# Row maxima of an attention kernel found bank by bank, its head projection taken out within one group, one product moved to GpSimd

## The chip, the cores and the metric

One core of a Trainium2 chip runs the whole program. The metric is the time of one execution in microseconds (us) of device time. The kernel before took 4465.28 us (median of three runs, 4464.08 to 4466.0). Engines are named PE (TensorE), PEld (its weight loads), DVE (VectorE), ACT (ScalarE), POOL (GpSimd) and SP (SyncE).

## The reference

A decoder layer in fp32 on x of shape (2, 2048, 512): self-attention, cross-attention to 77 rows, and a feed-forward block in which a router sends 512 rows of each batch through a larger network. The change lies in the self-attention, which is this:

```
x = x + attn(layernorm(x))
q, k, v = (h @ W.T).reshape(B, S, H, DK)        # H = 16 heads, DK = 64, S = 2048, B = 2
scores  = einsum('bhqd,bhkd->bhqk', q, k) + rel_bias[bucket(k - q)]
attn    = softmax(scores, axis=-1)
out     = einsum('bhqk,bhkd->bhqd', attn, v)  -> @ Wo.T
```

`rel_bias` is a table of 32 buckets by 16 heads. A key more than 128 columns before or after its query always falls in one of two buckets, so the bias is a constant there ("far"); nearer than that it varies ("near").

## The kernel before, in words

The program has three parts: `attention` (self-attention), `middle` (cross-attention and the light network), `routed` (the router and the heavy network). Only `attention` is changed. Each engine has its own instruction stream, written out by hand; semaphores tie them together. Nothing is reordered by a scheduler, so an instruction that waits holds up all that is behind it on its engine.

**Heads and groups.** Batch and head together make 32 units, called heads here, numbered 0 to 31. `heads` calls `head(n)` for n from -2 to 31 on every engine. A head is 32 steps (`STEPS`): two halves of 1024 queries, and in each the 16 tiles of 128 keys. Two steps make a group, so a head has 16 groups, g = 0 to 15. Three heads are in work at once: head n has its scores, exponentials and values; the row maxima of head n+1 are found in groups 3 to 15 of head n and the last three query tiles in groups 0 to 2 of the next; the projection of queries and keys of head n+2 is computed in four blocks of 512 columns, each over the groups 4b+1, 4b+2 and 4b+3. Head -2 so does only projection, head -1 projection and maxima.

**One group on PE** (`head` at L502) is, in order: score products "low" of step 2g, each with a product for a row maximum beside it (`row_tiles`, L472; low uses rows 64 to 127 of the array at L470, the maximum rows 0 to 63 at L455); "high" products of steps 2g and 2g+1 (L469; in groups 0 and 8 preceded by "first", L467, and there without low); a third of a projection block (L441, in three groups of four); low and maximum of step 2g+1; eight value products of the two steps before (L490, four matmuls of two instructions). Groups 4 and 12 end with the column sums of a finished half (`sum_of`, L499 and L500), which write the bank PB. The projection uses the same bank PB, so `sum_of` also waits until the block in it has been taken out (semaphore `step_lo`).

**Row maxima.** For each of 16 query tiles, four matmuls of 512 keys each give the raw scores, two at a time ("pair" 0 and 1 of a group) into the two banks MX and MX+1. DVE reduces both banks in one instruction of 1024 columns (`largest`, L726). PE's first matmul of the next pair waits for that reduction (`max_done`). `guards` (L728) makes of eight tiles' maxima the subtrahend of the softmax, `neg_max`, in two instructions (L732, L737); the second also subtracts the head's largest bias.

**Exponentials.** ACT waits for `scored`, and for near tiles for `biased`, which DVE's `near` (L747) signals; it writes `probs`, a ring of four steps. POOL adds `probs` into `acc` (L227, L230), 30 additions a head. PE's "high" of step 2g+1 waits for the exponential of step 2g-1.

**Taking out a projection block.** In groups 3, 7, 11 and 15, ACT copies the queries (`queries_out`, L598) between its two exponentials and the keys twice (`keys_out`, L602 and L603) after the second; DVE makes the queries' low part at the group's end (L753). In the group after it (4, 8, 12, 0), DVE forms the difference of keys two tiles apart (`step`, L759), ACT copies it (`step_hi`, L608), DVE makes its low part (`step_lo`, L765).

**Context.** When a half is done, its sums go through SP's DMAs to be inverted (`reciprocals`, L772, groups 13 and 5) and come back; DVE multiplies the context by them (`context`, L778, groups 14 and 6), and SP stores it.

Lines to follow: `row_tiles` and `max_half` (PE), `queries_out`, `keys_out`, `step_hi` (ACT), `largest`, `guards`, `step`, `step_lo`, `context` (DVE).

Of the kernel before, what the change touches and what calls it, by code (L numbers as in the profile page):

```python
# [71 lines left out]
CONTEXT_GROUPS = {14: 0, 6: 1}  # L72
# [11 lines left out]
def attention(nc, io, scr):  # L84

    with ExitStack() as c:
# [3 lines left out]
        def sem(name):  # L90
# [30 lines left out]
        maxes = sb("maxes", [P, NT, 2])  # L121
        max_q = sb("max_q", [P, NT])
# [20 lines left out]
        names = """const_ready consts_in bias_table bias_mm bias_stored wv_in wv_hi wv_lo stat  # L143
            moment rstd1 rstd2 xn turned xhi xlo vps vout w_in w_hi w_split
            proj q_hi k_own k_hi q_lo step step_hi step_lo fill_max fill_score
            maxed max_done neg1 neg_ready neg_stored neg_in
# [45 lines left out]
        def _(pool):  # L192
# [17 lines left out]

            def head(n, k, side):
# [6 lines left out]
                for st in range(STEPS):  # L218
                    qb, kt = divmod(st, NT)
                    if kt == 0:  # L220
                        continue
# [10 lines left out]
            heads(pool, head)  # L232

        @block.sync
        def _(sp):
# [28 lines left out]
            sp.wait_ge(s["bias_table"], 3)  # L264
# [123 lines left out]
        def _(pe):  # L388
# [57 lines left out]
            def max_half(n, side, g, pair, i):  # L446

                late, qt = max_tile(g)
                m, mside = (n + 1, 1 - side) if late else (n, side)
                if i == 0:  # L450
                    if late and g == FIRST_MAX and pair == 0:
                        pe.wait_ge(s["fill_max"], FILLS_MAX * (m + 1))
                    past(pe, s["max_done"], NT * 2 * m + 2 * qt + pair)
                kc = 2 * pair + i
                mm = pe.matmul(ps[:, MX + i, :], stacks[0:64, mside, QA, qt * P:(qt + 1) * P],  # L455
                               stacks[0:64, mside, KX, kc * 512:(kc + 1) * 512], start=True, stop=True)
                if i == 1:
                    mm.then_inc(s["maxed"], 1)
# [92 lines left out]
        def _(act):  # L551
            act.wait_ge(s["bias_mm"], 1)
            act.copy(rtab, ps[0:H, MX, :]).then_inc(s["bias_table"], 1)
# [37 lines left out]
            def queries_out(m, tb):  # L591
# [7 lines left out]

            def keys_out(m, tb):  # L600

# [38 lines left out]
            def head(n, k, side):  # L640
                carry, own, nxt, prep = parts(n)
                for g in range(GROUPS):
# [4 lines left out]
                    if prep and g in EVAC_GROUPS:  # L647
                        queries_out(n + 2, EVAC_GROUPS[g])
                    if g in SPLIT_GROUPS:
                        tb = SPLIT_GROUPS[g]  # L650
                        if tb < BLOCKS - 1 and prep:
                            step_hi(n + 2, tb)
                        if tb == BLOCKS - 1 and nxt:
                            step_hi(n + 1, tb)
                    if own:
                        exp(n, k, side, 2 * g + 1)
                    if prep and g in EVAC_GROUPS:
                        keys_out(n + 2, EVAC_GROUPS[g])
# [14 lines left out]
        def _(dve):  # L673
            dve.wait_ge(s["consts_in"], 48)
            dve.tensor_copy(rconst[:, 0:2], rb_t[:, FAR_AFTER:BUCKETS:BUCKETS // 2]).then_inc(s["bias_table"], 1)
            dve.memset(rconst[:, 3:4], 0.0)
            dve.tensor_reduce(rconst[:, 2:3], rb_t[:], AX.X, ALU.max).then_inc(s["bias_table"], 1)
# [42 lines left out]
            def largest(n, side, g, pair):  # L720
# [3 lines left out]
                at = NT * 2 * m + 2 * qt + pair  # L724
                dve.wait_ge(s["maxed"], at + 1)
                dve.tensor_reduce(maxes[:, qt, pair:pair + 1], ps[:, MX:MX + 2, :], AX.XY, ALU.max).then_inc(s["max_done"], 1)  # L726

            def guards(m, k, side, half):  # L728

                q = slice(half * 8, half * 8 + 8)  # L730
                dve.wait_ge(s["max_done"], NT * 2 * m + NT * (half + 1))
                dve.tensor_reduce(max_q[:, q], maxes[:, q, :], AX.X, ALU.max).then_inc(s["neg1"], 1)  # L732
                dve.wait_ge(s["neg1"], 2 * m + half + 1)
                if half == 0:
                    dve.wait_ge(s["far_in"][side], k * 16 + 16)
                past(dve, s["neg_stored"], 16 * (2 * m + half - 1))
                dve.tensor_scalar(neg_max[:, q], max_q[:, q], -1.0, far_bias[:, side, 2:3], ALU.mult, ALU.subtract).then_inc(s["neg_ready"], 1)  # L737
# [36 lines left out]
            def context(n, qb):  # L774

# [973 lines left out]
```

## Time and profile before

| | us |
|---|---|
| median of three runs | 4465.28 |
| the profiled execution | 4465.17 |
| its span, first to last instruction | 4463.4 |
| PE busy | 4052.3 (91%) |
| POOL busy | 2617.0 (59%) |
| DVE busy | 2602.8 (58%) |
| ACT busy | 2054.8 (46%) |
| granted TensorE clock, mean | 0.958 of full |

An engine's busy time is the time in which at least one of its instructions is in work. A matmul's recorded length holds its latency, so neighbouring ones overlap and the distance of two starts is what a matmul costs. Times in rows count from the span's start. The stretch in which heads 0 to 31 are worked on lasts from about 338 to 3122 us. A row of a timeline may stand for several instructions of one line (x2, x4), and then starts with the first and ends with the last.

### The profile page before, as it was taken

What the parts mean: (1) busy time and instruction counts of PE and PEld (TensorE: products, weight loads), DVE (VectorE), ACT (ScalarE), POOL (GpSimd) and SP (SyncE); (2) the same over time, 40 slices, a digit from 0 to 9 for tenths busy, and PEclk for the clock granted to TensorE, in tenths of its full rate; (3) what the DMA queues carried; (4) which work ended last, traced back from release to release, by engine and by line L of the source; (5) the groups of instructions that cost most, each with busy time, mean ns of one, the idle gap of its engine ahead of it and who ended that gap; (6) DMA issues with size and microseconds to landing.
All of it is one profiled execution on the core that took longest, in us unless ns stands there. A gap on an engine that the chain in (4) does not pass through costs nothing. (4 is left out here: it accounts for less than half of the span.)

```text
span 4463.4 us, 59267 instructions
## 1 busy us (share of the span) xinstructions
PE 4052.3 (91%) x18676; PEld 2172.5 (49%) x18676; DVE 2602.8 (58%) x3421; ACT 2054.8 (46%) x3407; POOL 2617.0 (59%) x1279
## 2 busy tenths in 40 slices
PE   8969999999999999999999999998588988883599
PEld 6734444444444444444444444443466666662244
DVE  3336666766766676666667667663256666653400
ACT  2215555555555555555555555554234444441110
POOL 1007888888888788888888888888222222220100
PEclk9969999999999999999999999999799999995799
DMA  6522222321222342122223212220311111112100
GB/s 195 147 69 60 72 55 58 93 57 52 81 72 54 111 115 58 52 76 75 57 55 97 57 52 79 71 54 15 116 46 53 53 47 59 47 33 88 38 10 10
DMA packets 340399, 299.90 MB, mean 67 GB/s; under 512 B 188779, under 2 KB 230251, under 8 KB 339304
## 3 DMA queue, kind: packets, MB, share of 16 engines
q1 hardware_dynamic: 272360, 275.94, 21.8%
q10 hardware_dynamic: 66048, 16.78, 1.7%
q0 software_dynamic: 1920, 6.29, 0.5%
q8 instruction: 38, 0.62, 0.1%
q14 instruction: 33, 0.27, 0.0%
HBM read 117.71 MB, written 64.54 MB: 41 GB/s over the span
## 5 line engine op out<-in xcount | busy, mean ns | idle before, releaser
L230 POOL TENSOR_TENSOR acc<-acc,probs 128x1024 f32<-128x1024 f32 x896 | 2148.6, 2398 | 353.7 <-ACT probs L634 215.5
L726 DVE TENSOR_REDUCE maxes<-ps 128x1 f32<-128x1024 f32 x1024 | 1250.5, 1221 | 650.7 <-PE ps L455 649.2
L637 ACT ACTIVATE probs<-ps,far_bias 128x1024 f32<-128x1024 f32 (+7 forms) x1280 | 1023.2, 820 | 1059.4 <-DVE near_s L747 552.4
L490 PE MATMUL ps<-probs,v_head 128*64 128x512 f32 x4096 | 997.0, 608 | 2.1 <-ACT probs L634 2.1
L455 PE MATMUL ps<-stacks 64*128 64x512 f32 x2048 | 759.8, 451 | 37.4 <-DVE maxes L726 37.4
L470 PE MATMUL ps<-stacks 64*128 64x512 f32 x1792 | 662.1, 447 | 0.0
L469 PE MATMUL ps<-stacks 128*128 128x512 f32 x2048 | 617.0, 418 | 0.1
L470 PEld LDWEIGHTS ps<-stacks 64*128 64x128 f32 x1792 | 271.0, 184 | 528.3 <-issue 358.6
L490 PEld LDWEIGHTS ps<-probs,v_head 128*64 128x64 f32 x4096 | 248.9, 136 | 484.1 <-issue 481.1
L469 PEld LDWEIGHTS ps<-stacks 128*128 128x128 f32 x2048 | 350.3, 188 | 215.6 <-issue 163.7
L747 DVE TENSOR_TENSOR near_s<-ps,near_bias 128x384 f32<-128x384 f32 (+2 forms) x576 | 284.1, 493 | 221.9 <-PE ps L470 205.4
L455 PEld LDWEIGHTS ps<-stacks 64*128 64x128 f32 x2048 | 306.8, 188 | 142.9 <-DVE maxes L726 105.5
L634 ACT ACTIVATE probs<-near_s 128x384 f32<-128x384 f32 (+2 forms) x576 | 271.1, 471 | 0.0
L441 PE MATMUL ps<-xn_hi,w_hi 128*128 128x512 f32 x512 | 211.3, 413 | 20.6 <-DVE c_k L765 15.8
L441 PE MATMUL ps<-xn_hi,w_lo 128*128 128x512 f32 x512 | 209.8, 410 | 0.0
L441 PE MATMUL ps<-xn_lo,w_hi 128*128 128x512 f32 x512 | 209.8, 410 | 0.0
L227 POOL TENSOR_TENSOR acc<-probs 128x1024 f32<-128x1024 f32 x64 | 152.9, 2388 | 81.5 <-ACT probs L637 64.9
L417 PE MATMUL ps<-stacks,xn_hi 128*128 128x512 f32 x512 | 163.8, 401 | 11.4 <-DVE xn_lo L703 11.4
L1011 POOL TENSOR_TENSOR m_rs<-m_rs,m_expo 128x1 f32<-128x1 f32 x32 | 17.6, 551 | 258.1 <-DVE m_rs L1245 258.1
L1019 POOL TENSOR_TENSOR m_rs<-m_rs,m_expo 128x1 f32<-128x1 f32 x32 | 17.6, 549 | 230.1 <-DVE m_rs L1245 230.1
L1000 POOL TENSOR_TENSOR m_ctx_lo<-m_ctx,m_ctx_hi 128x1024 fp32r<-128x1024 f32 x32 | 78.5, 2453 | 98.2 <-ACT m_ctx_hi L1176 98.2
L1421 POOL DMA_INDIRECT out<-r_y,index x8 | 7.8, 978 | 215.2 <-DVE r_y L1650 215.2
(222 smaller groups left out, 5046.7 us busy)
## 6 DMA issues: line engine op xcount, KB each, us to landing
stacks<-c_k SPq DMA_DIRECT2D x128, 256.0 KB, 2.4
stacks<-c_q SPq DMA_DIRECT2D x128, 256.0 KB, 2.5
stacks<-c_d SPq DMA_DIRECT2D x256, 128.0 KB, 2.3
scr_v<-c_k ACTq DMA_DIRECT2D x32, 512.0 KB, 4.0
stacks<-c_q SPq DMA_DIRECT2D x128, 128.0 KB, 2.3
v_head<-scr_v SPq DMA_DIRECT2D x32, 512.0 KB, 3.5
sums<-scr_inv SPq DMA_DIRECT2D x128, 128.0 KB, 2.9
scr_ctx<-ctx_out SPq DMA_DIRECT2D x128, 128.0 KB, 2.3
```

The costliest lines, as they stand in the source:

```text
L227: pool.tensor_tensor(acc[:, qb, :], probs[:, (st - 1) % PT_RING, :], pr, ALU.add).then_inc(s["summed"], 2)
L230: pool.tensor_tensor(acc[:, qb, :], acc[:, qb, :], pr, ALU.add).then_inc(s["summed"], 1)
L417: mm = pe.matmul(ps[:, 2 + v % 4, :], xs[i][:, k, t * P:(t + 1) * P], (wv_hi, wv_lo)[j][:, k, half * 512:(half + 1) * 512], start=at == 0, ...
L441: mm = pe.matmul(ps[:, PB, :], w[wi][:, kk, :], xs[xi][:, kk, tb * 512:(tb + 1) * 512], start=a == 0, stop=a == len(TERMS) - 1)
L455: mm = pe.matmul(ps[:, MX + i, :], stacks[0:64, mside, QA, qt * P:(qt + 1) * P], stacks[0:64, mside, KX, kc * 512:(kc + 1) * 512], start=T ...
L469: return pe.matmul(out, stacks[:, side, KA, keys], stacks[:, side, QA, q], start=False, stop=True, skip_group_check=True)
L470: return pe.matmul(out, stacks[64:128, side, KX, keys], stacks[64:128, side, QB, q], start=False, stop=True, skip_group_check=True)
L490: mm = pe.matmul(ps[64 * half:64 * half + 64, PV, :], v_head[:, side, kt, :], probs[:, st % PT_RING, half * 512:(half + 1) * 512], start=k ...
L634: ins = act.activation(probs[:, st % PT_RING, a:z], near_s[:, st % 2, 0:z - a], ACT.Exp)
L637: ins = act.activation(probs[:, st % PT_RING, a:z], sc[:, a:z], ACT.Exp, bias=bias)
L726: dve.tensor_reduce(maxes[:, qt, pair:pair + 1], ps[:, MX:MX + 2, :], AX.XY, ALU.max).then_inc(s["max_done"], 1)
L747: dve.tensor_tensor(near_s[:, st % 2, 0:z - a], sc, near_bias[:, side, j0:j0 + z - a], ALU.add).then_inc(s["biased"], 1)
```

## The change

Four things change, all in `attention`:

1. **Maxima bank by bank.** Every maximum matmul now signals `maxed` and waits for `max_done` of the matmul two before it, which used its bank. `largest` reduces each bank by itself (2048 reductions of 512 columns in place of 1024 of 1024). `guards` is one reduction over four partial maxima.
2. **The largest bias is taken off the tables.** The bias tables have it subtracted once at the start, so `guards` no longer subtracts it and its second instruction (L737) is gone.
3. **The projection is taken out within its group.** ACT does all three copies between its two exponentials and `step_hi` after the second; DVE does `step` right behind `queries_low` at the end of the same group, and `step_lo` between the two near steps of the next group.
4. **The product with the inverted sums is on POOL**, ahead of the addition of steps 30 and 14 (groups 15 and 7).

DVE, from the maxima of the end of group 3 (tile `maxes`) to those of the end of group 4, before: `c_q<-` is the queries' low part, `ps<-ps,c_d` is `step`, `c_k<-` is `step_lo`.

```order
L726 TENSOR_REDUCE maxes<-ps 128x1 [waits a_maxed]
L752 ISA
L753 TENSOR_TENSOR c_q<-ps,c_q 64x512 [waits a_q_hi]
L725 REGISTER_ALU
L726 TENSOR_REDUCE maxes<-ps 128x1 [waits a_maxed]
L743 REGISTER_ALU
L747 TENSOR_TENSOR near_s<-ps,near_bias 128x128 [waits a_scored]
L759 TENSOR_TENSOR ps<-ps,c_d 64x512 [waits a_q_lo,a_k_hi]
L725 REGISTER_ALU
L726 TENSOR_REDUCE maxes<-ps 128x1 [waits a_maxed]
L765 TENSOR_TENSOR c_k<-ps,c_d 64x512 [waits a_step_hi]
```

The same stretch of DVE in the changed kernel, from the second reduction at the end of group 3:

```order
L727 TENSOR_REDUCE maxes<-ps 128x1 [waits a_maxed]
L749 ISA
L750 TENSOR_TENSOR c_q<-ps,c_q 64x512 [waits a_q_hi]
L756 TENSOR_TENSOR ps<-ps,c_d 64x512 [waits a_q_lo,a_k_hi]
L726 REGISTER_ALU
L727 TENSOR_REDUCE maxes<-ps 128x1 [waits a_maxed]
L726 REGISTER_ALU
L727 TENSOR_REDUCE maxes<-ps 128x1 [waits a_maxed]
L740 REGISTER_ALU
L744 TENSOR_TENSOR near_s<-ps,near_bias 128x128 [waits a_scored]
L762 TENSOR_TENSOR c_k<-ps,c_d 64x512 [waits a_step_hi]
```

`step` has moved ahead of the next group's first maxima, and `step_lo` ahead of its last ones (two reductions, which follow).

ACT in groups 3 and 4, before, from the exponential of step 6: `c_q` is the queries' copy, the first `c_d` and the `c_k` the keys', `c_d` with its wait for `step` is `step_hi`.

```order
L634 ACTIVATE probs<-near_s 128x384
...
L598 CAST c_q<-ps 64x512 [waits a_fill_score]
...
L637 ACTIVATE probs<-ps,far_bias 128x768 [waits a_biased]
L634 ACTIVATE probs<-near_s 128x256
L602 COPY c_d<-ps 64x512
L603 CAST c_k<-ps 64x512
...
L637 ACTIVATE probs<-ps,far_bias 128x896 [waits a_biased]
L634 ACTIVATE probs<-near_s 128x128
L608 CAST c_d<-ps 64x512 [waits a_step]
```

And in the changed kernel:

```order
L639 ACTIVATE probs<-near_s 128x384
...
L606 CAST c_q<-ps 64x512 [waits a_fill_score]
L607 COPY c_d<-ps 64x512
L608 CAST c_k<-ps 64x512
...
L642 ACTIVATE probs<-ps,far_bias 128x768 [waits a_biased]
L639 ACTIVATE probs<-near_s 128x256
L613 CAST c_d<-ps 64x512 [waits a_step]
...
L642 ACTIVATE probs<-ps,far_bias 128x896 [waits a_biased]
L639 ACTIVATE probs<-near_s 128x128
```

Both key copies now stand ahead of the exponential of step 7, and `step_hi` ahead of that of step 8.

PE at the end of group 4, before and then changed: L470 and L477 are the low products, L455 and L464 the maxima beside them.

```order
L470 MATMUL ps<-stacks 128x512
L164 REGISTER_ALU
L455 MATMUL ps<-stacks 128x512 [waits a_max_done]
L470 MATMUL ps<-stacks 128x512
L455 MATMUL ps<-stacks 128x512
L490 MATMUL ps<-probs,v_head 64x512 x4
L496 REGISTER_ALU
L499 MATMUL ps<-acc,ones 64x512 [waits a_summed,a_sum_out,a_step_lo]
L500 MATMUL ps<-acc,ones 64x512
```

```order
L477 MATMUL ps<-stacks 128x512
L163 REGISTER_ALU
L464 MATMUL ps<-stacks 128x512 [waits a_max_done]
L477 MATMUL ps<-stacks 128x512
L163 REGISTER_ALU
L464 MATMUL ps<-stacks 128x512 [waits a_max_done]
L497 MATMUL ps<-probs,v_head 64x512 x4
L503 REGISTER_ALU
L506 MATMUL ps<-acc,ones 64x512 [waits a_summed,a_sum_out,a_step_lo]
L507 MATMUL ps<-acc,ones 64x512
```

The second maximum has a wait of its own now.

The diff, cut to its core:

```diff
 RECIP_GROUPS = {13: 0, 5: 1}
-CONTEXT_GROUPS = {14: 0, 6: 1}
+CONTEXT_STEPS = {30: 0, 14: 1}
 PART = 2 * 512 // P
...
+            def context(n, qb):
+
+                pool.wait_ge(s["recip_in"], 64 * n + 32 * qb + 32)
+                pool.wait_ge(s["ctx_raw"], 2 * n + qb + 1)
+                pool.tensor_tensor(ctx_out[:], ctx_out[:], sums[:], ALU.mult).then_inc(s["ctx"], 1)
+
             def head(n, k, side):
...
                     qb, kt = divmod(st, NT)
+                    if st in CONTEXT_STEPS:
+                        of = CONTEXT_STEPS[st]
+                        if of == 0 or carry:
+                            context(n if of == 0 else n - 1, of)
                     if kt == 0:
...
             heads(pool, head)
+            context(NH - 1, 1)
...
             norms(0, 1)
-            sp.wait_ge(s["bias_table"], 3)
+            sp.wait_ge(s["bias_table"], 2)
             sp.dma_start(scr["rtab"], rtab).then_inc(s["bias_stored"], 16)
...
                 m, mside = (n + 1, 1 - side) if late else (n, side)
-                if i == 0:
-                    if late and g == FIRST_MAX and pair == 0:
-                        pe.wait_ge(s["fill_max"], FILLS_MAX * (m + 1))
-                    past(pe, s["max_done"], NT * 2 * m + 2 * qt + pair)
                 kc = 2 * pair + i
-                mm = pe.matmul(ps[:, MX + i, :], stacks[0:64, mside, QA, qt * P:(qt + 1) * P],
-                               stacks[0:64, mside, KX, kc * 512:(kc + 1) * 512], start=True, stop=True)
-                if i == 1:
-                    mm.then_inc(s["maxed"], 1)
+                if late and g == FIRST_MAX and kc == 0:
+                    pe.wait_ge(s["fill_max"], FILLS_MAX * (m + 1))
+                past(pe, s["max_done"], NT * 4 * m + 4 * qt + kc - 1)
+                pe.matmul(ps[:, MX + i, :], stacks[0:64, mside, QA, qt * P:(qt + 1) * P],
+                          stacks[0:64, mside, KX, kc * 512:(kc + 1) * 512], start=True, stop=True).then_inc(s["maxed"], 1)
...
             act.wait_ge(s["bias_mm"], 1)
-            act.copy(rtab, ps[0:H, MX, :]).then_inc(s["bias_table"], 1)
+            act.wait_ge(s["bias_max"], 1)
+            act.activation(rtab, ps[0:H, MX, :], ACT.Identity, bias=rconst[:, 2:3]).then_inc(s["bias_table"], 1)
             act.wait_ge(s["wv_in"], 16)
...
-            def queries_out(m, tb):
+            def take_out(m, tb):
...
                 act.copy(c_q[0:64, cols].bitcast(F32R), ps[0:64, PB, :]).then_inc(s["q_hi"], 1)
-
-            def keys_out(m, tb):
-
                 act.copy(c_d[64:128, LOOKBACK + tb * 512:LOOKBACK + (tb + 1) * 512], ps[64:128, PB, :]).then_inc(s["k_own"], 1)
...
                     if prep and g in EVAC_GROUPS:
-                        queries_out(n + 2, EVAC_GROUPS[g])
-                    if g in SPLIT_GROUPS:
-                        tb = SPLIT_GROUPS[g]
-                        if tb < BLOCKS - 1 and prep:
-                            step_hi(n + 2, tb)
-                        if tb == BLOCKS - 1 and nxt:
-                            step_hi(n + 1, tb)
+                        take_out(n + 2, EVAC_GROUPS[g])
                     if own:
...
                     if prep and g in EVAC_GROUPS:
-                        keys_out(n + 2, EVAC_GROUPS[g])
+                        step_hi(n + 2, EVAC_GROUPS[g])
                     if g == 0 and carry:
...
             dve.wait_ge(s["consts_in"], 48)
-            dve.tensor_copy(rconst[:, 0:2], rb_t[:, FAR_AFTER:BUCKETS:BUCKETS // 2]).then_inc(s["bias_table"], 1)
             dve.memset(rconst[:, 3:4], 0.0)
-            dve.tensor_reduce(rconst[:, 2:3], rb_t[:], AX.X, ALU.max).then_inc(s["bias_table"], 1)
+            dve.tensor_reduce(rconst[:, 2:3], rb_t[:], AX.X, ALU.max, negate=True).then_inc(s["bias_max"], 1)
+            dve.wait_ge(s["bias_max"], 1)
+            dve.tensor_scalar(rconst[:, 0:2], rb_t[:, FAR_AFTER:BUCKETS:BUCKETS // 2], rconst[:, 2:3], None, ALU.add).then_inc(s["bias_table"], 1)
             dve.wait_ge(s["wv_hi"], 1)
...
                 m = n + 1 if late else n
-                at = NT * 2 * m + 2 * qt + pair
-                dve.wait_ge(s["maxed"], at + 1)
-                dve.tensor_reduce(maxes[:, qt, pair:pair + 1], ps[:, MX:MX + 2, :], AX.XY, ALU.max).then_inc(s["max_done"], 1)
-
-            def guards(m, k, side, half):
+                for i in range(2):
+                    kc = 2 * pair + i
+                    dve.wait_ge(s["maxed"], NT * 4 * m + 4 * qt + kc + 1)
+                    dve.tensor_reduce(maxes[:, qt, kc:kc + 1], ps[:, MX + i, :], AX.X, ALU.max).then_inc(s["max_done"], 1)
+
+            def guards(m, half):
...
                 q = slice(half * 8, half * 8 + 8)
-                dve.wait_ge(s["max_done"], NT * 2 * m + NT * (half + 1))
-                dve.tensor_reduce(max_q[:, q], maxes[:, q, :], AX.X, ALU.max).then_inc(s["neg1"], 1)
-                dve.wait_ge(s["neg1"], 2 * m + half + 1)
-                if half == 0:
-                    dve.wait_ge(s["far_in"][side], k * 16 + 16)
+                dve.wait_ge(s["max_done"], NT * 4 * m + 2 * NT * (half + 1))
                 past(dve, s["neg_stored"], 16 * (2 * m + half - 1))
-                dve.tensor_scalar(neg_max[:, q], max_q[:, q], -1.0, far_bias[:, side, 2:3], ALU.mult, ALU.subtract).then_inc(s["neg_ready"], 1)
+                dve.tensor_reduce(neg_max[:, q], maxes[:, q, :], AX.X, ALU.max, negate=True).then_inc(s["neg_ready"], 1)
...
                 dve.reciprocal(part_inv[:], part[:]).then_inc(s["recip"], 1)
-
-            def context(n, qb):
-
-                dve.wait_ge(s["recip_in"], 64 * n + 32 * qb + 32)
-                dve.wait_ge(s["ctx_raw"], 2 * n + qb + 1)
-                dve.tensor_tensor(ctx_out[:], ctx_out[:], sums[:], ALU.mult).then_inc(s["ctx"], 1)
...
                     if stepped:
-                        step(*stepped)
+                        step_lo(*stepped)
                     if own:
...
                         largest(n, side, g, 1)
-                    if stepped:
-                        step_lo(*stepped)
                     if prep and g in EVAC_GROUPS:
                         queries_low(n + 2, EVAC_GROUPS[g])
+                        step(n + 2, EVAC_GROUPS[g])
                     if g == FIRST_MAX + NT // 2 - 1 and nxt:
-                        guards(n + 1, k + side, 1 - side, 0)
+                        guards(n + 1, 0)
                     if g == LAST_MAX and own:
-                        guards(n, k, side, 1)
-                    for groups, act_on in ((RECIP_GROUPS, reciprocals), (CONTEXT_GROUPS, context)):
-                        if g in groups:
-                            qb = groups[g]
-                            if own if qb == 0 else carry:
-                                act_on(n if qb == 0 else n - 1, qb)
+                        guards(n, 1)
+                    if g in RECIP_GROUPS:
+                        qb = RECIP_GROUPS[g]
+                        if own if qb == 0 else carry:
+                            reciprocals(n if qb == 0 else n - 1, qb)
...
             reciprocals(NH - 1, 1)
-            context(NH - 1, 1)
     return all_of(s)
```

## Rows read from the trace of the kernel before

**Rows 1.** Windows: stretch, length, busy us of PE, PEld, DVE, ACT, POOL, clock, DMA.

```profile
278.90:350.60 71.70, 49.60 (x91) 24.85 (x92) 38.84 (x39) 9.65 (x17) 1.27 (x1) 0.50 0.16 37
1741.90:1828.90 87.00, 85.71 (x382) 40.04 (x381) 59.51 (x71) 50.26 (x82) 73.92 (x33) 1.00 0.25 69
```

**Rows 2.** Timeline of PE, head 17, groups 5 and 6: start, length, instruction, [idle before].

```profile
1854.77 1.20 PE L469 MATMUL ps<-stacks 128*128 128x512 f32 x4
...
1859.37 0.49 PE L470 MATMUL ps<-stacks 64*128 64x512 f32 x1
1859.37 0.49 PE L455 MATMUL ps<-stacks 64*128 64x512 f32 x1
...
1860.03 1.19 PE L469 MATMUL ps<-stacks 128*128 128x512 f32 x4
```

**Rows 3.** Timeline of PE, head 17, group 4.

```profile
1848.63 1.20 PE L469 MATMUL ps<-stacks 128*128 128x512 f32 x4
1849.76 0.50 PE L470 MATMUL ps<-stacks 64*128 64x512 f32 x1
1850.03 0.50 PE L455 MATMUL ps<-stacks 64*128 64x512 f32 x1
...
1850.36 0.39 PE L455 MATMUL ps<-stacks 64*128 64x512 f32 x1
1850.69 1.94 PE L490 MATMUL ps<-probs,v_head 128*64 128x512 f32 x8
1853.10 0.64 PE L499 MATMUL ps<-acc,ones 128*64 128x512 f32 x1 [0.47 <-DVE c_k L765]
```

**Rows 4.** Waits, 338 to 2943 us: total, times, longest.

```profile
PE ps L499 <- DVE c_k L765: 39.4, 59, 0.9
```

**Rows 5.** Timeline of DVE, head 17, group 11.

```profile
1885.54 2.36 DVE L737 TENSOR_SCALAR neg_max<-max_q,far_bias 128x8 fp32r<-128x8 f32 x1 [0.25 <-DVE max_q L732]
```

**Rows 6.** Timeline of PE, head 17, group 11.

```profile
1888.32 0.50 PE L470 MATMUL ps<-stacks 64*128 64x512 f32 x1
1889.08 0.50 PE L455 MATMUL ps<-stacks 64*128 64x512 f32 x1 [0.27 <-DVE maxes L726]
```

**Rows 7.** Line L737 alone: count, ns least/median/most.

```profile
L737 DVE TENSOR_SCALAR neg_max<-max_q,far_bias x64: 231/825/2465, 318.7 to 3051.5; 128x8 fp32r<-128x8 f32 x64
```

**Rows 8.** Groups by line: count | busy us, mean ns | idle before and releaser.

```profile
L726 DVE TENSOR_REDUCE maxes<-ps 128x1 f32<-128x1024 f32 x1024 | 1250.5, 1221 | 650.7 <-PE ps L455 649.2
...
L778 DVE TENSOR_TENSOR ctx_out<-ctx_out,sums 128x512 f32<-128x512 f32 x64 | 83.4, 1303 | 17.9 <-DMA sums<-scr_inv 17.1
L737 DVE TENSOR_SCALAR neg_max<-max_q,far_bias 128x8 fp32r<-128x8 f32 x64 | 79.1, 1236 | 9.3 <-DVE max_q L732 3.5
...
L215 POOL TENSOR_TENSOR w_lo<-w_in,w_hi 128x512 fp32r<-128x512 f32 x32 | 40.7, 1272 | 140.5 <-ACT w_hi L589 140.5
```

**Rows 9.** Timeline of DVE, head 17, groups 3 and 4.

```profile
1847.79 0.68 DVE L753 TENSOR_TENSOR c_q<-ps,c_q 64x512 fp32r<-64x512 f32 x1
1848.75 1.23 DVE L726 TENSOR_REDUCE maxes<-ps 128x1 f32<-128x1024 f32 x1 [0.27 <-PE ps L455]
...
1849.89 0.28 DVE L747 TENSOR_TENSOR near_s<-ps,near_bias 128x128 f32<-128x128 f32 x1
```

**Rows 10.** Timeline of ACT, head 17, group 3.

```profile
1846.54 0.57 ACT L598 CAST c_q<-ps 64x512 fp32r<-64x512 f32 x1
1847.01 0.90 ACT L637 ACTIVATE probs<-ps,far_bias 128x768 f32<-128x768 f32 x1
1847.80 0.41 ACT L634 ACTIVATE probs<-near_s 128x256 f32<-128x256 f32 x1
```

**Rows 11.** Timeline of PE in head -1.

```profile
296.38 1.22 PE L455 MATMUL ps<-stacks 64*128 64x512 f32 x2 [1.32 <-DVE maxes L726]
...
302.07 0.79 PE L455 MATMUL ps<-stacks 64*128 64x512 f32 x1 [1.32 <-DVE maxes L726]
```

**Rows 12.** Waits, 3028 to 3125 us (head 31).

```profile
PE ps L499 <- POOL acc L230: 5.5, 1, 5.5
```

More of the change, by code:

```diff
@@ L120, in attention @@
         ones = sb("ones", [P, DK])
-        maxes = sb("maxes", [P, NT, 2])
-        max_q = sb("max_q", [P, NT])
+        maxes = sb("maxes", [P, NT, 4])
         neg_max = sb("neg_max", [P, NT], F32R)
@@ L141, in attention @@
         SC, PV, PB, MX = 0, 4, 5, 6
-        names = """const_ready consts_in bias_table bias_mm bias_stored wv_in wv_hi wv_lo stat
+        names = """const_ready consts_in bias_max bias_table bias_mm bias_stored wv_in wv_hi wv_lo stat
             moment rstd1 rstd2 xn turned xhi xlo vps vout w_in w_hi w_split
             proj q_hi k_own k_hi q_lo step step_hi step_lo fill_max fill_score
-            maxed max_done neg1 neg_ready neg_stored neg_in
+            maxed max_done neg_ready neg_stored neg_in
             scored biased exped summed pved summ sum_out spread recip recip_stored recip_in
```

## The prediction

> **What bounds the kernel now.** I read the busy times first, then windows, then the timeline of one head engine by engine, then the waits. In a full head PE is busy 85.7 of 87.0 us at the full clock, DVE 59.5, ACT 50.3, POOL 73.9 [rows 1]. PE is the bound, so only time in which PE stands still can be won. In a plain group its starts of "high" lie 5.26 us apart, and the low product and the maximum beside it start at the same 0.01 us, though that maximum carries a wait [rows 2]. Five groups of sixteen are longer than their matmuls. In group 4 the first maximum starts 0.27 after its low product, because the reduction before is not done, and the sums start 2.41 after the first value product; 1.87 would do, so they wait 0.54 [rows 3]. The same two waits stand in group 12. The recorded idle before the sums is 39.4 us in 59 cases, and about 0.07 of each start is hidden behind the last matmul's tail [rows 4]: 43.5 us in all. In group 11 one maximum starts 0.76 after its low product [rows 6], behind a DVE instruction on 128x8 values that took 2.36 us [rows 5] where its shortest took 0.23 [rows 7]. Groups 7 and 15 are longer mainly by the "first" products, which stay.
>
> Head -1 is another stage: PE at half clock, busy 49.6 of 71.7 us [rows 1], and idle 1.32 us ahead of each pair of maxima that follows a pair directly [rows 11]. At the end POOL is late: PE waits 5.5 us for its last addition [rows 12].
>
> **Part 1, maxima bank by bank.** 1024 reductions of 1024 columns at 1.22 us [rows 8] become 2048 of 512. No row shows one. The near additions and the queries' low part give it: 0.28 for 128 columns [rows 9], 0.68 for 512, so 0.13 per 128 columns and 0.15 fixed; I take 0.69. The bounds are 0.61 (half of the long one) and 0.76 (0.15 more fixed cost than half). Two in a row: in the row before, 0.08 of an instruction overlaps the next (1848.75 to 1849.89 for 1.23 us), so a pair is 1.29, at worst 1.41. DVE gains 32 x 0.07 to 0.19 = 2 to 6 us of work a head, beside 27 idle ones.
>
> What it gives PE: the first matmul of a pair needs only the first bank's reduction, the second only the second's. What it costs is told with part 3, since both meet in groups 4, 12 and 0. PE has 1024 more waits and 1024 more signals, and behind a waiting maximum stand all its later products. Where the wait is already met I take its cost at 0, since the waiting maximum of rows 2 starts with its neighbour; the upper bound is the second rival's.
>
> The skill has a rule against this. The Trainium skill, "TensorE: Matmul & The Clock Gate", section on the per-tile semaphore tail, puts 26 ns on each increment by a matmul and advises one on the last tile only. By it 1024 more increments would cost an estimated 27 us. In rows 2 and 3 the maximum that signals (the second of a pair) is followed by the next matmul 0.33 us on, as its silent partner is (1850.03 to 1850.36, 1850.36 to 1850.69); the trace disagrees as far as it shows.
>
> **Part 2, the largest bias off the tables.** L737 goes, 79.1 us of DVE [rows 8]. Its mean is 1236 ns for 64. Half of them (group 2) lie near the median 0.83, which leaves 52.7 us for the 32 of group 10; between 0.23 and 2.4 that is 21 slow ones [rows 7]. Each delays PE by 0.76 [rows 6]: 21 x 0.76 = 16 us. The one reduction left works on 32 values a row and waits for nothing else on PE's path; at worst it takes the 0.23 of the shortest L737. The tables at the start are 16 rows on engines that wait for a weight load: nothing.
>
> **Part 3, projection out within its group.** Gains: `step_lo` comes ahead of group 4's last maxima, so the sums no longer wait: the 43.5 us. Costs, worked out in group 3 to 4 of head 17. DVE: the last maxima of group 3 end 0.07 later, the queries' low part runs 1847.86 to 1848.54 (it was 1847.79), `step` at 0.70 (by the 0.68 of its size) to 1849.27, and only then the first maxima of group 4, which began at 1848.75 [rows 9]: 1849.30 to 1849.99, and 1849.90 to 1850.59. PE's first maximum goes at 1850.0 as now (1850.03), the second at 1850.61 in place of 1850.36 [rows 3]: 0.25 lost. In group 12 the near step before is 128 wide in place of 256 and DVE is 0.1 earlier: 0.14 lost. 30 heads x 0.39 = 12 us; with the pair at 1.41 it is 19. In group 0 DVE is late too, but PE has no low product there and reaches its next maxima when they are free: 0, at worst 0.15 x 30 = 4.5.
>
> ACT: exponential 7 now starts after three copies. The first starts at 1846.54 and they take 0.57 each, 1.7 together, so it runs 1848.2 to 1849.4, where it ended at 1848.21 [rows 10]. PE wants it for the third product of 1848.63, about 1849.2. It loses some 0.25, but stands waiting for the maxima until 1850.0 anyway. If DVE were not late, this would be the next stall. `step_hi` waits for `step` at 1849.27, and queued behind it is exponential 8, which waits for its near step until about 1850.8: covered.
>
> **Part 4, the product on POOL.** DVE loses 83.4 us. On POOL a product of this size took 1.27 us [rows 8], so POOL goes from 73.9 to 76.5 us of 87. The inverted sums have landed when DVE wants them in group 14 (11 waits, 17.1 us in all), and POOL comes to them in group 15. Behind it on POOL stand the additions, then the weight split for the next projection. I count 0 for the heads to 29, and 1.5 us gained on DVE in group 15. In heads 30 and 31, with no projection, POOL is the bound: its 60 additions and four products come to about 156 us behind the first exponential, and PE's stalls in head 30 vanish; I take 4 us gained (0 to 7). The last product stands on the path: 1.27 for some 0.68 (DVE's operation on 64x512, [rows 9]), 0.6 us lost.
>
> **Head -1.** Between two pairs that follow directly, PE waits 1.32 us, at half clock 2.54 from pair to pair. With banks apart the round is one matmul (0.79), 0.05 and 0.69: some 1.6. Thirteen groups have 15 such places: 15 x 0.93 = 14 us. Between 8 (some behind the copies) and 40 (the clock rises).
>
> **Sum.** 43.5 - 12 + 16 + 1.5 + 4 - 0.6 + 14 = 66.4 us. The profiled execution took 4465.17 (span 4463.4), the median 4465.28, so the trace stands for it: 4465.2 - 66.4 = 4399 us.
>
> **Rivals.**
> - *The clock rises in head -1.* PE goes from 69% busy to over 80% there. At 2.4 GHz DVE's four reductions (2.8) and one copy (0.6) set a group, about 3.4 us, in place of the 4.8 that stay at 1.2 GHz (71.7 / 13 less 0.7 to 0.9). For it: full heads, 98% busy, hold the full clock. Against: 71.7 us at half clock without a break. 13 x 1.5 to 2 = 20 to 27 more: 4374.
> - *Signals and waits cost on PE.* A maximum's second weight load cannot go until its own wait is looked at. For it: two more register instructions a group pair on PE's stream. Against: rows 2. At 0.03 us for each signal with its wait, 1024 x 0.026 to 0.03 is 27 to 31 us; I take 27: 4426. By the Trainium skill's rule named above the time would come out there too. Rows 2 and 3 are printed to 0.01 us, so a cost of two or three such steps is the most that they leave open.
> - *The stalls only move.* DVE does about 9.0 us of work in groups 3 and 4 and is 1 us late at the border. If its reductions take 0.76 and `step` waits for the key copies, each of the four borders loses 0.5 more: 4 x 0.5 x 30 = 60 us, and the time is 4459, no change.
> - *Slower: the second maximum no longer starts beside its low product.* In each of 28 second pairs a head, PE would run low and maximum one after the other, as in the first pair of rows 3, 0.27 us each: 28 x 0.27 x 30 = 227 us, 4399 + 227 = 4626. It decides when the wait of the second load is met later than its neighbour's start. For it: DVE finishes the second bank up to 0.6 us after the first. Against: outside groups 4 and 12 more than 1.5 us lie between a reduction's end and the next use of its bank; the first maxima meet their waits in just this way.
>
> **How the numbers follow.** Forecast 0.56 (own range 4383 to 4425, from the bounds: pair 1.41, group 0, head -1 at 8 on one side, fewer losses in groups 4 and 12 and 7 us at the end on the other); clock 0.15; signals 0.12; stalls move 0.09; pairing lost 0.08. The range 4366 to 4446 leaves out the last two and a tail of the clock's. A measurement here can tell 0.2% from no change, 8.9 us. Faster: 0.56 + 0.15 + 0.12 and 0.01 of the fourth, 0.84; within 0.2%: 0.06; slower: 0.10.
>
> **What would show it.** Right: a plain group still 5.26; group 11 always 5.26; no wait of the sums for `step_lo`; the reduction 0.69; group 4 from 6.14 (1848.63 to 1854.77, [rows 2, 3]) to about 5.85, its second maximum 0.6 behind the first; head -1 about 14 us shorter; POOL 76.5 a head. Wrong, if the low product and the second maximum start apart in plain groups, if PE waits for the exponential in groups 4, 12 or 0, or if POOL's product holds additions back.

## The result: 0.15% slower, where 1.5% faster was forecast

The changed kernel takes 4472.59 us (median of 20 runs, 4467.97 to 4477.0), the kernel before, measured beside it, 4465.99 (20 runs): a ratio of 1.0015, 95% interval 1.0008 to 1.0022. The forecast was 4399 and its range ended at 4446. Both numbers come out of one trace: most of the gains are there, and in every second head from head 3 to head 27 they are paid back.

Three stretches of the changed kernel: length, busy us of PE, PEld, DVE, ACT, POOL, granted clock, DMA. Head 16; group 0 of head 17; the rest of head 17.

```profile
1741.47:1826.89 85.42, 85.23 (x378) 39.74 (x377) 57.65 (x99) 50.11 (x79) 75.06 (x34) 1.00 0.25 68
1826.89:1836.72 9.83, 7.63 (x22) 2.78 (x20) 4.61 (x9) 4.10 (x7) 6.42 (x4) 0.69 0.83 272
1836.72:1917.55 80.83, 80.65 (x358) 37.80 (x357) 53.13 (x91) 46.13 (x72) 68.53 (x31) 1.00 0.17 39
```

Head 16 takes 85.42 us where a head took 87.0 [rows 1]. Head 17 takes 9.83 + 80.83 = 90.66. Of the 5.2 us that it has over head 16, 4.9 are in its group 0, which takes 4.90 elsewhere, and 0.3 in the group behind it. There PE is idle 2.2 us and the granted clock is 0.69 on average: from 1830.61 to 1837.43, from the end of the idle time on, PE ran at 1.2 GHz. PE's waits of the changed kernel, 345 to 2960 us (total, times, longest):

```profile
PE ps L464 <- DVE maxes L727: 27.9, 13, 2.2
PE ps L476 <- ACT probs L639: 3.1, 1, 3.1
```

The sums' 59 waits [rows 4] are gone, as forecast. The 13 new ones are the 13 long heads (groups 0 of 7.6 to 9.9 us, median 8.93). The timeline of PE, then of DVE there (start, length, instruction, [idle before <- what ended it]):

```profile
1830.63 1.39 PE L464 MATMUL ps<-stacks 64*128 64x512 f32 x2 [2.20 <-DVE maxes L727]
```

```profile
1825.55 0.68 DVE L750 TENSOR_TENSOR c_q<-ps,c_q 64x512 fp32r<-64x512 f32 x1
1826.33 0.70 DVE L756 TENSOR_TENSOR ps<-ps,c_d 64x512 f32<-64x512 f32 x1
1829.89 1.29 DVE L727 TENSOR_REDUCE maxes<-ps 128x1 f32<-128x512 f32 x2 [2.85 <-issue]
1831.21 0.42 DVE L744 TENSOR_TENSOR near_s<-ps,near_bias 128x256 f32<-128x256 f32 x1
```

"issue" is the word to see: DVE stands 2.85 us, the maxima that it would reduce are long there, and no semaphore ends the wait. In the trace's list of all of DVE's instructions, the loop's branch stands at 1826.43 and the next one, a register operation, at 1829.76. The loop over heads holds two heads and is run 14 times, so 13 branches are taken. Before, the loop's first instruction came 0.31 us behind the branch; now 3.1 to 3.4. From branch to branch DVE ran 259 instructions, now 391: the reductions doubled, and each wait in the loop brings register arithmetic along. The code's own transfers show it too, the queue of kind "instruction" between 900 and 2600 us, first before, then after:

```profile
q14 instruction: 3, 0.02, 0.0%
```

```profile
q14 instruction: 52, 0.43, 0.1%
```

1700 us are 9.7 turns of the loop: five packets of 8192 bytes each turn, where the kernel before loaded nothing for DVE. Its three packets stand in every run, 128 instructions of SP apart, so they are SP's. The durations that the sum rested on came out right; the rows of after that answer to [rows 8], the wait at the end that answers to [rows 12], and head -1 as in [rows 11]:

```profile
L727 DVE TENSOR_REDUCE maxes<-ps 128x1 f32<-128x512 f32 x2048 | 1316.0, 684 | 637.7 <-PE ps L464 594.5 <-issue 36.5
L214 POOL TENSOR_TENSOR ctx_out<-ctx_out,sums 128x512 f32<-128x512 f32 x64 | 81.9, 1279 | 11.2 <-DMA sums<-scr_inv 11.2
```

```profile
PE ps L506 <- POOL acc L239: 4.6, 1, 4.6
```

```profile
306.76 1.22 PE L464 MATMUL ps<-stacks 64*128 64x512 f32 x2
308.34 1.39 PE L464 MATMUL ps<-stacks 64*128 64x512 f32 x2 [0.36 <-DVE maxes L727]
```

In the first row, 36.5 us of the reductions' idle time end in "issue": 13 x 2.8.

### The profile page after: what moved, and what is told of

Read it like the earlier page. It is cut to its first block and busy times, and to the rows that moved or that the text cites. A ratio compares the mean times of both kernels' runs of the same rounds, so it can differ in the third digit from the quotient of the medians.

```text
span 4474.0 us, 62747 instructions
## 1 busy us (share of the span) xinstructions
PE 4087.9 (91%) x18676; PEld 2186.4 (49%) x18676; DVE 2522.6 (56%) x4317; ACT 2076.4 (46%) x3407; POOL 2675.4 (60%) x1343
## 5 line engine op out<-in xcount | busy, mean ns | idle before, releaser
L727 DVE TENSOR_REDUCE maxes<-ps 128x1 f32<-128x512 f32 x2048 | 1316.0, 684 | 637.7 <-PE ps L464 594.5
L497 PE MATMUL ps<-probs,v_head 128*64 128x512 f32 x4096 | 1018.2, 619 | 4.3 <-ACT ctx_out L625 4.3
L464 PE MATMUL ps<-stacks 64*128 64x512 f32 x2048 | 793.0, 461 | 47.1 <-DVE maxes L727 40.4
L477 PE MATMUL ps<-stacks 64*128 64x512 f32 x1792 | 659.6, 447 | 0.0
L477 PEld LDWEIGHTS ps<-stacks 64*128 64x128 f32 x1792 | 271.0, 186 | 539.4 <-issue 353.4
L464 PEld LDWEIGHTS ps<-stacks 64*128 64x128 f32 x2048 | 317.5, 189 | 174.2 <-DVE maxes L727 145.7
```

What stands on the lines that cost most here:

```text
L477: return pe.matmul(out, stacks[64:128, side, KX, keys], stacks[64:128, side, QB, q], start=False, stop=True, skip_group_check=True)
L497: mm = pe.matmul(ps[64 * half:64 * half + 64, PV, :], v_head[:, side, kt, :], probs[:, st % PT_RING, half * 512:(half + 1) * 512], start=k ...
L727: dve.tensor_reduce(maxes[:, qt, kc:kc + 1], ps[:, MX + i, :], AX.X, ALU.max).then_inc(s["max_done"], 1)
```

## Experiments

Theory A: DVE's code in the loop is no longer held on the engine, so each taken branch waits for a load. Its rivals are named in each expectation. The runs come from three sessions of four kernels, and each ratio is against the kernel before in the same session (medians of 4463.73, 4465.28 and 4466.69).

**The loop taken away.**

```
-            with engine.Fori(0, NH // 2 - 2) as j:
+            for j in range(NH // 2 - 2):
```

> The changed kernel with heads 1 to 28 written out one after the other, in place of a loop of two heads that is run 14 times; each head's work is the same. Theory A (code loading: DVE's loop body grew from 259 to 391 instructions, and at each of the 13 taken branches DVE stands 3.1 to 3.3 us with nothing to run, which PE pays with some 4.2): no branch, so no gap; every head 85.4 us, the whole some 55 us below the changed kernel, 4415 to 4422. Rival B (the wait in group 0 of every other head is work or a wait of its own place, such as the step that moved into the group before): the long heads of 89 to 90.7 us stay, 4465 to 4475.

Measured: 4417.03 us, ratio 0.9898 (0.9883 to 0.9913). Heads 1 to 29 but 13 and 14 take 85.4 us. Theory A; B is out, since the same order of work has no long heads. Here code is loaded all along, and not for DVE alone, between 900 and 2600 us:

```profile
q8 instruction: 59, 0.97, 0.2%
q14 instruction: 51, 0.42, 0.1%
```

Held against each engine's own count of instructions, the 51 packets of q14 are those of ACT, DVE and POOL (one for each 128 instructions of each, about 17 of them DVE's) and SP's three. The 59 of q8 have 16384 bytes, one for each 256 or so recorded instructions of PE. Outside heads 13 and 14 every head is as long as the others, though packets come in all of them: loading in sequence cost nothing that shows, the jump is what costs.

**The parts apart.** First the changed kernel with maxima in pairs again (below its DVE part; PE too waits and signals once a pair), then part 1 alone on the kernel before.

```
-                for i in range(2):
-                    kc = 2 * pair + i
-                    dve.wait_ge(s["maxed"], NT * 4 * m + 4 * qt + kc + 1)
-                    dve.tensor_reduce(maxes[:, qt, kc:kc + 1], ps[:, MX + i, :], AX.X, ALU.max).then_inc(s["max_done"], 1)
+                dve.wait_ge(s["maxed"], NT * 2 * m + 2 * qt + pair + 1)
+                dve.tensor_reduce(maxes[:, qt, pair:pair + 1], ps[:, MX:MX + 2, :], AX.XY, ALU.max).then_inc(s["max_done"], 1)
```

> The changed kernel with the row maxima found in pairs of banks again (one wait and one reduction of 1024 columns a pair); parts 2 to 4 of the change stay. DVE's loop body is 241 instructions. Theory A: no gap at the branch; the sums' waits and the 21 waits of group 11 are gone as in the changed kernel, head -1 keeps its 79 us, 4405 to 4425. Rival B (the place, not the number of instructions): the long heads stay, 4460 to 4475. Theory C (the bank-wise signals cost PE and DVE all over): 4400 or less, with plain groups under 5.25 us.

> The kernel before with part 1 of the change alone: maxima bank by bank. DVE's loop body is 409 instructions. Theory A: 13 gaps of 3.2 us on DVE at the branch, which lies in group 0 of every other head, some 55 us on PE, less 5 in head -1: 4505 to 4525. Rival B (it needs the moved step): no such gap, 4450 to 4470.

Measured: pairs 4433.29, ratio 0.9933 (0.9919 to 0.9946), no long head, 85.67 a head. It is 8 us over the range of theory A, which I had put too low. Against the kernel without the loop, bank-wise maxima are worth 16 us, 9 of them in head -1 (head 0 begins at 349.82 for 340.85). Part 1 alone: 4449.64, ratio 0.9968 (0.9957 to 0.9979), far under theory A's 4505 to 4525 and just below B's range. But the gap is there (DVE of that kernel, head 9):

```profile
1115.74 0.69 DVE L751 TENSOR_TENSOR c_q<-ps,c_q 64x512 fp32r<-64x512 f32 x1
1119.04 1.29 DVE L724 TENSOR_REDUCE maxes<-ps 128x1 f32<-128x512 f32 x2 [2.61 <-issue]
```

```profile
1119.78 1.09 PE L454 MATMUL ps<-stacks 64*128 64x512 f32 x2 [1.15 <-DVE maxes L724]
```

```profile
1117.08:1123.65 6.57, 5.32 (x22) 2.27 (x20) 4.52 (x8) 4.10 (x9) 3.90 (x3) 1.00 0.39 146
```

The second fence is PE's first maximum of that head, the third its group 0 as a whole: 6.57 us where 4.65 is normal, at the full clock. From the branch (1115.52) to the next instruction it is 3.4 us. The branch stands 1.56 us ahead of the head's first "high", in the changed kernel only 0.46: there the step is one more instruction of DVE ahead of the branch. So nearly the same gap on DVE costs PE 1.9 in one kernel (1.15 of them idle) and 4.0 in the other (median; 2.0 to 2.3 idle, most of the rest at 1.2 GHz). The two parts together cost more than each alone. That the place of the branch makes this difference is read from the two traces; no run moves the branch by itself. My expectation had priced the gap by its cost in another kernel. The kernel also gains what its banks give: 9.4 us by head 0's first "high" (339.11 for 348.55), and 9.0 behind head 30's (1500.9 for 1509.9).

**Only code added.** The kernel before, with two, then one unused instruction behind each reduction in the loop:

```
+                if not isinstance(n, int) and True:
+                    for c in range(2):
+                        at = side * 128 + g * 8 + pair * 4 + c
+                        dve.memset(junk[:, at:at + 1], 0.0)
```

> The kernel before, and behind each row-maximum reduction in the loop two DVE instructions that set one unused value a row; they add 128 instructions to DVE's loop body (387 in place of 259) and nothing else is changed. Theory A: gaps of 3.2 us behind 13 branches; PE loses some 4 us at each, 4505 to 4520. Rival B: nothing at the branch; at most some tenths of a us in groups where DVE is late, 4465 to 4480.

> The kernel before with one of the two unused settings behind each reduction: half the added work, DVE's loop body 323 instructions. Theory A (code loading has a step: it costs nothing while the body is held, and 3.2 us of DVE a branch when it is not): no code is loaded inside the loop and nothing is lost at the branch, 4461 to 4470. Rival D (each added instruction costs in proportion, or it is the settings' own time): half of the 44 us that 128 of them cost, 4480 to 4492.

Measured: with 387 instructions 4507.84, ratio 1.0103 (1.0088 to 1.0119): theory A. With 323, where I expected nothing, 4502.2, ratio 1.0089 (1.0075 to 1.0102), and the gap and the 52 packets are there. In both the branch stands 1.5 us ahead of "high", and PE is idle 1.5 to 2.1 us behind it. Rival D is no better: half the instructions cost not half but nearly all (37 us of 44). A plain limit on their number was wrong as well, as the next run but one shows, whose body of 327 is free.

**Controls.** The kernel before without its loop, by the same edit as above; and the changed kernel with its loop and one wait a pair:

```
+                dve.wait_ge(s["maxed"], NT * 4 * m + 4 * qt + 2 * pair + 2)
                 for i in range(2):
                     kc = 2 * pair + i
-                    dve.wait_ge(s["maxed"], NT * 4 * m + 4 * qt + kc + 1)
```

> The kernel before with heads 1 to 28 written out. Theory A: its body of 259 instructions is held and its branch is followed at once, so there is nothing to win: 4455 to 4468. Rival E (loops cost on their own, by register arithmetic or the branches of the other engines, and the 57 us that the changed kernel won were that): 4400 to 4430.

> The changed kernel, still with its loop, where DVE waits once a pair (for its second bank) and then reduces the two banks apart; PE still signals each bank and waits for each. DVE's loop body is 327 instructions. Theory A: the gaps at the branch go, 55 us; the first reduction starts 0.33 us later where DVE is late (groups 0, 4 and 12), up to 0.3 x 3 x 30 = 27 us of it lost: 4417 to 4445. Rival B: gaps stay, 4470 or more.

Measured: 4460.88, ratio 0.9994 (0.9985 to 1.0003): a loop whose code is held costs nothing that can be told, so the 55 us were no general price of loops. One wait a pair: 4421.28, ratio 0.9901 (0.9886 to 0.9916), heads of 85.4, no gap, 3 packets. Within heads the later first reduction costs nothing; in head -1 and head 30 it costs some 5 us together.

**The step taken back.** Without the loop, `step` and `step_hi` go back into the group behind, as in the kernel before; `step_lo` stays ahead of the last maxima.

> The changed kernel written out without its loop (4417 us), and the step taken back behind the next group's first maxima, as in the kernel before, but with its low part still ahead of the last maxima. Theory F (the 0.25 of group 0, 0.25 to 0.6 of group 4 and 0.5 of group 12 above their matmuls are DVE's lateness behind the step): group 0 back to 4.65, groups 4 and 12 shorter by 0.1 to 0.3, 10 to 20 us less: 4397 to 4408. Rival G (the low part then comes late again for the sums): up to 0.5 a sum, 4417 to 4445.

Measured: 4432.72, ratio 0.9928 (0.9915 to 0.9942), 16 us worse than without this edit. Group 4 fell (5.91 to 5.73), but group 0 rose from 4.90 to 5.40: DVE's low part then waits 0.50 us for ACT, and four reductions stand behind it.

```profile
776.96 0.68 DVE L766 TENSOR_TENSOR c_k<-ps,c_d 64x512 fp32r<-64x512 f32 x1 [0.50 <-ACT c_d L613]
777.68 2.57 DVE L731 TENSOR_REDUCE maxes<-ps 128x1 f32<-128x512 f32 x4
```

Theory F misread group 0. Rival G's range held, but not its place: the sums wait 0.3 us each (29 waits, 9.7 us), and the groups that end with them change by -0.18 (4) and +0.05 (12).

**Where the code lies.** 327 instructions were held and 323 were not. In the trace a code packet comes when DVE is 114, 244 and 375 instructions behind the branch in the changed kernel, whose loop begins 336 instructions into DVE's code; 46, 171 and 301 behind it in the kernel with 323, whose loop begins at 282. In DVE's code these are the same places, and the kernels with 387 and 409 instructions have them too: about 325 to 328, 447 to 453, 577 to 583 and 708 to 711, blocks of 128 instructions (8192 bytes). (Places are counted in the code; the trace records three or four instructions fewer ahead of the loop. That shifts borders and bodies alike.) 336 to 663 touches three of them, 282 to 605 touches four. The test moves the second body by 49 instructions that run once ahead of the loop (of the 50 settings written, the trace has 49):

```
             dve.wait_ge(s["lead"], 1)
+            for c in range(50):
+                dve.memset(junk[:, 200 + c:201 + c], 0.0)
```

> The kernel of the run with 323 instructions in DVE's loop body (4502 us), with 49 further unused settings on DVE ahead of the loop, once, so that the same body lies 49 places later in DVE's code: at 331 to 654 in place of 282 to 605. From the moments at which code is loaded I put the borders of its blocks at about 324, 452, 580 and 708 (128 apart). Theory H (what counts is how many blocks the body touches: three are held, four are not): the body now touches three, no code is loaded in the loop, no gap, 4463 to 4475. Rival D' (the settings in the body cost their time, or the number of instructions decides): 4495 to 4510 as before.

> The changed kernel where, inside the loop and in groups 5, 6 and 9 alone, DVE waits once a pair and not for each bank: 12 instructions fewer, its body is 379, at 336 to 715. Theory H: it still touches a fourth block (border about 708), so the gaps stay: 4466 to 4476. Rival D'' (the cost goes with the number of instructions): 12 of the 132 added, some 5 us less, 4466 to 4470, and no sudden fall in the next run either.

> As the run before, with one wait a pair in groups 5, 6, 8, 9, 10, 13 and 14 inside the loop: DVE's body is 363, at 336 to 699, 16 instructions less than in the run before. Theory H: three blocks, no gap at the branch, no code loaded in the loop: 4412 to 4422. Rival D'': 10 to 12 us less than the changed kernel, 4460 to 4466.

The two others are the changed kernel with one wait a pair in three and in seven groups of the loop. Measured: shifted 4474.56, ratio 1.0017 (1.0008 to 1.0026), 28 us less than the same body in the wrong place, and no gap at any branch (8 us stay above the kernel before, 4 of them in head 1; most of the rest is that heads that took 86.2 us take 87.0, which no run explains); 379 instructions 4471.53, ratio 1.0009 (1.0000 to 1.0018); 363 instructions 4418.57, ratio 0.9890 (0.9874 to 0.9905). Sixteen instructions of 379 are worth 53 us. Code packets from 900 to 2600 us in these three, in this order:

```profile
q14 instruction: 3, 0.02, 0.0%
```

```profile
q14 instruction: 52, 0.43, 0.1%
```

```profile
q14 instruction: 3, 0.02, 0.0%
```

And DVE at the branch of the kernel with 363, to be held against the changed kernel's above:

```profile
1799.84 0.70 DVE L758 TENSOR_TENSOR ps<-ps,c_d 64x512 f32<-64x512 f32 x1
1800.57 1.29 DVE L729 TENSOR_REDUCE maxes<-ps 128x1 f32<-128x512 f32 x2
```

All ten kernels with a loop up to here fit: 282 to 541 (before), 278 to 519 (pairs), 336 to 663, 331 to 654 and 336 to 699 touch three blocks and load nothing; 282 to 605, 282 to 669, 336 to 715, 336 to 727 (changed) and 340 to 749 touch four and load five packets a turn.

**The best version.** The changed kernel with one wait a pair in the loop and, for the first key block, `step` back in group 4; below the part on DVE, ACT's `step_hi` of that block moves likewise.

```
-                        step_lo(*stepped)
+                        (step if g == 4 else step_lo)(*stepped)
...
+                    if stepped and g == 4:
+                        step_lo(*stepped)
...
-                        step(n + 2, EVAC_GROUPS[g])
+                        if g != 3:
+                            step(n + 2, EVAC_GROUPS[g])
```

> Meant as the best version: the changed kernel with one wait a pair inside the loop (DVE's body 327, at 336 to 663), and with the step of the first key block alone back behind group 4's first maxima. Theory H: no gap. Theory F' (from the run with the step moved for all four blocks, where group 4 fell from 5.91 to 5.73 and group 0 rose from 4.90 to 5.40): group 4 5.73, group 0 stays 4.90, 0.18 x 30 = 5 us below the run with one wait a pair: 4408 to 4416. Rival: group 4 gains nothing when the first reduction waits for the second bank, 4415 to 4422.

Measured: 4416.46, ratio 0.9887 (0.9872 to 0.9902), 1.1% faster than the kernel before and 1.3% than the changed one. It is at the edge of theory F' and in its rival's range: group 4 is 5.82 in every other head and 5.92 in the rest, and the 2 us to 4418.57 are less than these four runs of each can tell. Its DVE loads nothing in the loop.

## Why the prediction was wrong

The step that failed is in part 1: "DVE gains 32 x 0.07 to 0.19 = 2 to 6 us of work a head, beside 27 idle ones". It priced DVE's new instructions by their busy time. What they cost is their place in the code: the loop's body grew past what is held, and the branch back then waits 3.1 to 3.4 us, 13 times, which cost PE 56 us. No term of the sum and no rival stood for it. With this term taken out (the kernel with 363 instructions) the change gives 48 us of the forecast 66.

The Trainium skill, "Runtime: NRT & Kernel Launch", section "Instruction fetch mechanics", has the rule: a taken branch whose target is not in the held window forces a load before execution goes on. The runs agree. It gives blocks of 16 KiB and a window of two for most engines. PE's packets have that size here (16384 bytes), DVE's are 8192 bytes, and a DVE body over three of them was held and one over four was not, so for DVE the measurement decides on the size.

Point by point, with the measured terms (us of the whole; groups from "high" to "high" in heads without a branch, medians, where two kinds of heads differ their mean):

| step | forecast | measured |
|---|---|---|
| groups 4 and 12: sums' waits, later second maxima | 43.5 - 12 = 31.5 | 6.09 to 5.90, 6.56 to 5.76: 0.99 x 30 = 30 |
| group 0 | 0, at worst -4.5 | 4.65 to 4.90: -7.5 |
| group 11 | 16 | mean 5.75 to 5.26: 15 |
| group 15 | 1.5 | 5.88 to 5.82: 2 |
| head -1 | 14 (8 to 40) | head 0 begins 8.5 earlier |
| heads 30, 31 and the last product | 4 - 0.6 | 4.1 without the loop (1505.8 for 1509.9) |
| branches | not seen | 13 x 4.3 = -56 |

The measured terms, with nothing for the end, come to 8 us lost, and a disturbance in heads 13 and 14 took 3 more than before: 11. The two profiled executions differ by 10.6 (4474.0 for 4463.4), the medians by 6.6.

- Right: the reduction's 0.684 us for 0.69, the product's 1.28 for 1.27, plain groups still 5.26, group 11 without its stall, no waits of the sums; the rivals "signals and waits cost on PE" (85.4 us a head with 2048 signals, 85.7 with 1024) and "pairing lost" fell. One bound was added up wrongly: two reductions of 0.76 less 0.08 are 1.44, not 1.41; nothing hangs on it, since the pair took 1.29.
- Group 0 was mis-sized: I held that PE reaches its next maxima when they are free. PE in head 16:

```profile
1745.80 0.39 PE L477 MATMUL ps<-stacks 64*128 64x512 f32 x1
1745.94 0.49 PE L464 MATMUL ps<-stacks 64*128 64x512 f32 x1
```

  The second maximum starts 0.14 behind its low product: the reduction that it waits for ends at 1745.88.
- Head -1: a pair that follows directly comes 1.58 us behind the one before, as forecast, where no copy lies between on DVE, and 2.03 where one does; the pair after a piece of projection moved from 3.15 to 3.32, which the term of 15 x 0.93 left out. The clock stayed at half, so that rival fell.
- The time is nearest to "the stalls only move" (4459), but by luck: groups 4 and 12 did get shorter, and the mechanism is another.
- At the end the changed kernel itself gained nothing (1510.2 us behind head 30's first "high" for 1509.9), nor did the one with 379 instructions (1510.4), though all the changed ones without a gap did (1504.2 to 1506.9). In the changed kernel, of the 81 us of head 31 up to its last group, 24 ran at 1.2 GHz, and 14 in the one without the loop. Why these differ, no run isolates.

ACT's body of 361 instructions was never reloaded, though it is longer than a body of DVE that was. The kernel without the loop shows where its blocks lie: packets come when ACT has run 355, 480, 607, 737 and 862 instructions and so on, one every 128. By the same count the loop of the changed kernel is 489 to 849, so ACT's body touches three blocks, and the rule for DVE would hold it too. In the kernel before it is 482 to 843 and begins so near a border that the packets don't tell on which side. PE's body of 1730 recorded instructions was not reloaded either (no packet on q8 in the loop); where it would end being held, no run shows.

Open: a disturbance of some 2 to 8 us in heads 13 and 14 stands in every kernel, whatever the change.

## What to carry to other kernels

Before adding instructions or waits to an engine inside a loop, count that engine's instructions from branch to branch, and where they begin, and look at the profile's row for the queue of kind "instruction": if its packets are many more than the program's length needs, an engine loads its loop again each turn. From the blocks found here, up to 257 instructions of DVE touch no more than three blocks wherever they begin, and up to 384 can if they begin well. Here the cure was to merge 28 waits (391 to 363) or to write the loop out; for a padded body of 323 it was enough to move it. When two halves of a change each look harmless, ask what they share: here part 1 made the gap, and by the traces the moved step brought the branch to where PE felt more of it.

## What the hardware showed that I had not expected

- A taken branch of DVE cost about 0.3 us to the next instruction while the body touched three blocks of 128 instructions, and 2.9 to 3.8 when it touched four; five packets of 8192 bytes were then loaded each turn.
- With the loop written out, 51 packets of 8192 bytes (ACT, DVE, POOL, SP) and 59 of 16384 (PE) were loaded in 1700 us with no wait that shows.
- In the changed kernel PE stood still 2.0 to 2.3 us at each of the 13 branches. In 12 heads the clock fell to 1.2 GHz behind it, for 3.4 or 6.8 us, and group 0 took 8.7 to 9.9 us; in head 3 it did not, and the group took 7.6. With 0.9 to 1.2 us of idle time (part 1 alone) it fell in 2 heads of 13.
